# A two-layer attention and mixture-of-experts kernel: one slab's experts weighed on ScalarE out of PSUM, halved inverse sums stacked, and the steps put in another order without a loop

## The reference

```python
bias = einsum('bijd,dh->bhij', ln(x), Wb)                 # 4 heads, same for every row r
q, k, v = (ln(x) @ W).reshape(b, n, n, h, dh)             # W = Wq, Wk, Wv; dh = 32
sim = einsum('brihe,brjhe->brhij', q, k) * dh**-0.5 + bias[:, None]
attn = softmax(where(mask, sim, -1e9))
o = einsum('brhij,brjhe->brihe', attn, v)
x = x + (o * sigmoid(ln(x) @ Wg)) @ Wo
t = tokens(x)
p = softmax(ln(t) @ router_w + router_b)
top_p, top_i = top_k(p, 2);  top_p /= sum(top_p)
t = t + sum_k top_p[k] * (ln(t) @ expert_w[top_i[k]] + expert_b[top_i[k]])
```

## Time and profile before

| what | value |
|---|---|
| median of 3 runs | 878.78 us (878.75 to 878.98) |
| the profiled execution's own time | 878.26 us |
| its span, first to last instruction | 876.5 us |
| busy share of the span: PE, PEld, DVE, ACT, POOL | 92%, 61%, 86%, 57%, 74% |
| phase 1 and tables | 0 to about 97.8 us |
| first and last `exponent` of part 0 | 109.52 and 805.10 us |
| granted TensorE clock, 828 to 876.5 us | 0.51 of full speed |

### The profile page before, as it was taken

The page is one execution under the profiler, slowest core; times in us unless marked ns, Lnnn a source line. Parts: engine busy times, 40 slices in busy tenths (PEclk is TensorE's granted clock), DMA queues, the critical chain, the costliest instruction groups (busy, mean ns, idle before and its releaser), DMA issues.

```text
span 876.5 us, 40872 instructions
## 1 busy us (share of the span) xinstructions
PE 802.0 (92%) x15532; PEld 534.2 (61%) x15532; DVE 753.1 (86%) x1818; ACT 500.5 (57%) x1049; POOL 644.2 (74%) x1029
## 2 busy tenths in 40 slices
PE   1999679999999999999999999999999999999643
PEld 1899345666666666666666666666666666666411
DVE  8998545899999999999899998999999999998754
ACT  3887245655665566655665566655565566665220
POOL 6995002487788877887788878888788877888786
PEclk9999999999999999999999999999999999999955
DMA  4563100111110100101011100101011100100000
GB/s 118 193 200 137 39 25 22 37 39 35 34 56 30 37 30 30 52 30 37 30 45 37 37 30 30 52 30 37 30 44 38 37 30 30 52 25 18 17 15 16
DMA packets 32461, 40.82 MB, mean 47 GB/s; under 512 B 6288, under 2 KB 27280, under 8 KB 32400
## 3 DMA queue, kind: packets, MB, share of 16 engines
q1 hardware_dynamic: 31920, 39.95, 14.0%
q10 hardware_dynamic: 480, 0.02, 0.0%
HBM read 13.74 MB, written 6.55 MB: 23 GB/s over the span
## 4 chain that ended last, share of the span: by engine, by line
PE 67%; POOL 11%; issue 10%; DVE 9%; ACT 2%; DMA 0%; POOLq 0%; DVEq 0%
PE psS L1117 11%; PE psS L1092 6%; PE psS L1124 5%; DVE rinv L841 3%; POOL ln_s L375 3%; PE ps_x L1174 3%; PE ps_m L1174 3%; PE psS L1136 2%; PE ps_x L1177 2%; PE psS L1097 2%; PE ps_m L1177 2%; PE ps_o L1249 2%; POOL xn L378 2%; PE ps_x L1148 2%; PE ps_x L1250 2%
## 5 line engine op out<-in xcount | busy, mean ns | idle before, releaser
L825 DVE TENSOR_REDUCE negm<-psS 128x12 f16<-128x1920 f32 x80 | 145.7, 1821 | 16.2 <-PE psS L1097 9.0
L428 POOL TENSOR_TENSOR add<-prod 128x256 f32<-128x256 f32 x160 | 116.9, 730 | 4.3 <-DVE prod L943 2.1
L375 POOL TENSOR_TENSOR ln_s<-ln_s,half 128x5 f32<-128x5 f32 (+1 forms) x60 | 86.2, 1436 | 37.1 <-DVE ln_s L881 29.7
L433 POOL TENSOR_TENSOR add<-add 128x128 f32<-128x128 f32 x200 | 92.0, 460 | 3.1
L394 POOL TENSOR_TENSOR xc<-x,ln_s 128x320 f32<-128x320 f32 x40 | 29.3, 731 | 87.9 <-DVE ln_s L874 87.9
L545 ACT ACTIVATE pt_a<-psS 128x1280 f32<-128x1280 f32 x40 | 49.5, 1238 | 67.5 <-PE psS L1126 67.5
L545 ACT ACTIVATE pt_b<-psS 128x1920 f32<-128x1920 f32 x40 | 70.8, 1771 | 13.8 <-PE psS L1136 13.7
L435 POOL TENSOR_TENSOR ymix<-add 128x64 f32<-128x64 f32 x200 | 64.1, 321 | 15.7
L1092 PE MATMUL psS<-bm,ident 128*128 128x480 f16 (+1 forms) x320 | 68.0, 335 | 6.6 <-ACT pt_b L545 2.1
L416 POOL TENSOR_TENSOR og_lo<-og,og_hi 128x320 f16<-128x320 f32 x80 | 63.4, 793 | 10.5 <-ACT og_hi L582 9.9
L1117 PE MATMUL psS<-bt_hi,ident 128*128 128x320 f16 (+1 forms) x320 | 67.7, 334 | 3.3 <-issue 2.6
(11 more groups left out here) (267 smaller groups left out, 2921.2 us busy)
## 6 DMA issues: line engine op xcount, KB each, us to landing
xin<-in_x SPq DMA_DIRECT2D x20, 320.0 KB, 3.0
xs_all<-xs_pair SPq DMA_DIRECT2D x20, 320.0 KB, 2.5
xs_q<-xs_all SPq DMA_DIRECT2D x40, 160.0 KB, 2.1
xs_v<-xs_all SPq DMA_DIRECT2D x40, 160.0 KB, 2.1
xin<-in_x SPq DMA_DIRECT2D x40, 160.0 KB, 2.2
out<-res SPq DMA_DIRECT2D x40, 160.0 KB, 1.8
w_raw<-in_expert_w SPq DMA_DIRECT2D x2, 128.0 KB
eb_raw<-in_expert_b SPq DMA_DIRECT2D x15, 2.0 KB
```

Of the source, the lines that this page charges most:

```text
L375: pool.tensor_tensor(ln_s[a][:, 3, 0:w], ln_s[a][:, 2, 0:w], half[:, 0:w], ALU.pow).then_inc(own, 1)
L428: pool.tensor_tensor(add1[t % 2][:], prod_of(t)[:, 0:4, :], prod_of(t)[:, 4:8, :], ALU.add).then_inc(mix_step[t], 1)
L433: pool.tensor_tensor(add2[t % 2][:], add1[t % 2][:, 0:2, :], add1[t % 2][:, 2:4, :], ALU.add).then_inc(mix_step[t], 1)
L825: dve.tensor_reduce(negm[c][:, :, 0:slots], psS[:, :, 0:slots * N].rearrange("i h (s j) -> i h s j", s=slots), AX.X, ALU.max, negate=True) ...
```

## The change

**Slab 2.** `keep_expert` is gone. ACT's new `weigh_kept` reads the PSUM bank of slab 2 itself: eight activations (one per expert, 64 columns each) with the share `coef[:, 2, e]` as scale, a column of one value per partition. It waits for `share` 5, as POOL's did. POOL's multiply of `kept` is gone. The factor 1/16 now sits in `coef` (`share` 1 multiplies by 16 before the reciprocal), so `weigh` becomes a plain product and `share` 6 and 7 multiply by 16.

**Inverse sums.** `row_one` and `rest_one` have each row's ones twice, so `row_sums` gives each sum on two partitions. `rinv_high` is two activations, `rinv_s = sign * rinv` and `rinv_u = upper * rinv` (per-partition scales), and `rinv_low` one subtraction, `rinv_hl = rinv_u - rinv_s`: the tile has high halves on some partitions and low halves on others. `row_to_all` has ones at both, so `spread_inverse` is two matmuls for two rows instead of four. Its constants cost one more select on POOL, eight more small fills and three more small instructions on DVE, once.

**Order.** All five `step` lists are new, with other banks and offsets; steps -2 to 44 are all written out, without a loop, and there is one more step at the end. SP loads xs_q one step earlier and stores one step later.

```diff
-        FIRST, LOOP, LOOP_END, LAST = -2, 7, GROUPS - 3, GROUPS + 4
+        FIRST, LAST = -2, GROUPS + 5
-            for n in range(FIRST, LOOP):
-                step(n, n % 2)
-            pairs_loop(eng, step, LOOP, LOOP_END)
-            for n in range(LOOP_END, LAST):
+            for n in range(FIRST, LAST):
                 step(n, n % 2)
...
-                if third_on(n + 3): load_xq(n + 3, b)
+                if third_on(n + 4): load_xq(n + 4, a)
-                if on(n - 4): store(n - 4, a)
+                if on(n - 5): store(n - 5, b)
...
             def rinv_low(g):
                 pool.wait_ge(rh_done, g + 1)
-                pool.tensor_tensor(rinv_lo[:], rinv[:], rinv_hi[:], ALU.subtract).then_inc(rl_done, 1)
+                for c in range(2):
+                    need(pool, rb_done[c], g)
+                pool.tensor_tensor(rinv_hl[:], rinv_u[:], rinv_s[:], ALU.subtract).then_inc(rl_done, 1)
-            def weigh_kept(g, t):
-                pool.wait_ge(kept_done[t], g + 1)
-                pool.wait_ge(rt_tail, 7 * g + 5)
-                pool.tensor_tensor(kept[:], kept[:], coef[:, t, :].unsqueeze(2).broadcast_to([P, E, D]),
-                                   ALU.mult).then_inc(prod_done[t], 1)
...
             def rinv_high(g):
-                act.activation(rinv_hi[:], rinv[:], ACT.Copy).then_inc(rh_done, 1)
+                act.activation(rinv_s[:], rinv[:], ACT.Copy, scale=sign[:, 0:1])
+                act.activation(rinv_u[:], rinv[:], ACT.Copy, scale=upper[:, 0:1]).then_inc(rh_done, 1)
...
-            def keep_expert(g, t, bank):
+            def weigh_kept(g, t, bank):
                 act.wait_ge(e_done[t], g + 1)
+                act.wait_ge(rt_tail, 7 * g + 5)
...
-                act.activation(kept[:], bank[:].rearrange("p (e c) -> p e c", e=E), ACT.Copy, scale=1.0 / UP).then_inc(kept_done[t], 1)
+                for e in range(E):
+                    i = act.activation(kept[:, e, :], bank[:, D * e:D * e + D], ACT.Copy, scale=coef[:, t, e:e + 1])
+                i.then_inc(prod_done[t], 1)
...
+                prep(dve.tensor_reduce(upper[:], fold[:, 0:RG], AX.X, ALU.add))
+                prep(dve.tensor_scalar(sign[:], upper[:], -2.0, 1.0, ALU.mult, ALU.add))
+                prep(dve.tensor_scalar(upper[:], upper[:], -1.0, 1.0, ALU.mult, ALU.add))
...
             def spread_inverse(g, c, bank):
-                    mm(o, lhsT=row_to_all[:, 2 * c + s, :], rhs=rinv_hi[:], start=True, stop=False)
-                    end = mm(o, lhsT=row_to_all[:, 2 * c + s, :], rhs=rinv_lo[:], start=False, stop=True)
+                    end = mm(o, lhsT=row_to_all[:, 2 * c + s, :], rhs=rinv_hl[:], start=True, stop=True)
...
             def experts(g, a, t, bank):
-                take(bank, kept_done[t] if t in KEPT else prod_done[t], g + 1)
+                take(bank, prod_done[t], g + 1)
```

More of the change, by code:

```diff
@@ L1267, in step @@
                 b = 1 - a
-                if not isinstance(n, int) or n == LOOP_END:
-                    last[id(psS)] = max_done[1], n + 1
-                    last[id(ps_o)] = lg_done, n - 2
-                    last[id(ps_r)] = prod_done[3], n - 3
-                    last[id(ps_m)] = qkl_done[0][1], n + 2
-                    last[id(ps_x)] = qkl_done[1][1], n + 2
-                if on(n): scores(n, a, 0)
-                if on(n - 4): experts(n - 4, a, 4, ps_o)
-                if on(n): turn_max(n, 1, ps_r)
@@ L1278, in step @@
-                if later(n + 1): project_qk(n + 1, b, 0, 0, ps_m)
-                if on(n - 1): attend(n - 1, b, 1, ps_x)
-                if on(n - 4): turn_coef(n - 4, ps_o, banks16[0])
-                if on(n + 1): max_scores(n + 1, b, 0)
-                if on(n): project_v_rest(n, a, ps_r)
-                if on(n - 1): attend(n - 1, b, 0, ps_m)
-                if on(n + 1): project_gate(n + 1, b, 1, ps_x)
-                if on(n - 2): project_out(n - 2, ps_o)
-                if on(n + 1): project_gate(n + 1, b, 0, ps_r)
@@ L1287, in step @@
-                if on(n - 3): experts(n - 3, b, 2, ps_x)
-                if on(n): scores(n, a, 1)
-                if on(n - 4): expert_bias(n - 4, ps_m)
-                if on(n - 1): spread_inverse(n - 1, 1, ps_r)
-                if on(n - 3): experts(n - 3, b, 0, ps_x)
-                if on(n - 3): experts(n - 3, b, 1, ps_o)
-                if on(n): project_v(n, a, ps_m)
-                if on(n - 1): spread_inverse(n - 1, 0, ps_r)
+                if on(n): scores(n, a, 0)
+                if on(n - 1): attend(n - 1, b, 0, ps_x)
@@ new lines, in step @@
+                if on(n): turn_max(n, 1, ps_o)
+                if on(n - 5): expert_bias(n - 5, ps_r)
+                if on(n + 1): max_scores(n + 1, b, 0)
+                if on(n - 2): project_out(n - 2, ps_x)
+                if on(n + 1): project_gate(n + 1, b, 0, ps_o)
+                if on(n - 4): turn_coef(n - 4, ps_m, banks16[3])
+                if on(n - 1): attend(n - 1, b, 1, ps_r)
+                if on(n + 1): project_v_rest(n + 1, b, ps_o)
+                if on(n - 1): spread_inverse(n - 1, 0, ps_m)
@@ new lines, in step @@
+                if on(n): scores(n, a, 1)
+                if on(n - 1): spread_inverse(n - 1, 1, ps_o)
+                if on(n - 3): experts(n - 3, b, 1, ps_x)
+                if on(n - 3): experts(n - 3, b, 0, ps_m)
+                if on(n - 3): experts(n - 3, b, 2, ps_r)
+                if on(n - 3): experts(n - 3, b, 3, ps_o)
+                if on(n): row_sums(n, a, ps_x)
+                if later(n + 2): project_qk(n + 2, a, 0, 0, ps_m)
+                if on(n + 1): turn_max(n + 1, 0, ps_r)
@@ L1295, in step @@
+                if on(n + 1): project_gate(n + 1, b, 1, ps_o)
                 if on(n + 1): max_scores(n + 1, b, 1)
+                if on(n - 2): turn2(n - 2, a, ps_r, banks16[2])
+                if on(n): project_v(n, a, ps_x)
+                if on(n - 3): experts(n - 3, b, 4, ps_o)
+                if on(n - 2): router(n - 2, a, ps_r)
                 if later(n + 2): project_qk(n + 2, a, 1, 0, ps_m)
-                if on(n): row_sums(n, a, ps_x)
-                if on(n + 1): turn_max(n + 1, 0, ps_r)
@@ L1299, in step @@
-                if on(n - 2): turn2(n - 2, a, ps_o, banks16[0])
-                if later(n + 2): project_qk(n + 2, a, 0, 1, ps_m)
-                if on(n - 3): experts(n - 3, b, 3, ps_r)
-                if later(n + 2): project_qk(n + 2, a, 1, 1, ps_x)
-                if on(n - 2): router(n - 2, a, ps_o)
+                if later(n + 2): project_qk(n + 2, a, 0, 1, ps_x)
+                if later(n + 2): project_qk(n + 2, a, 1, 1, ps_r)
             pe.wait_ge(wb_ready, 1)
```

146 lines of the change are left out of this document (74 added, 72 removed).

## The result

The changed kernel takes **858.41 us** in the median of four runs (858.04 to 860.74); the kernel before, run beside it, 878.88 (878.75 to 879.07). The ratio is 0.9771, 95% interval 0.9756 to 0.9787: faster by 20.5 us. The forecast was 862.3 (854 to 875), so the direction and the range held and the size was 3.9 us short.

A forecast was written before the change was run, and what follows sets the result against it. The prediction took TensorE to bound phase 2, VectorE 1.3 us a step behind. Its terms, -3.7 - 9.9 - 9.2 + 10.8 - 2.2 + 0 - 3.0 + 0.7 = -16.5, gave a median of 862.3 us, range 854 to 875.

The forecast's parts named there:

- 4 new waits: TensorE waits at router for keep_xs2, second gate for slab 3's bank, row_sums for exponent: together 0.30 us a step, +10.8.
- 5 shapes: Changes of TensorE's array shape, with two joints no row shows: -0.06 us a step, -2.2, ends -3 and +4.5.
- 6 slab 2: Eight scaled activations on ScalarE take 1.8 us; turn_max waits for their bank with room up to 1.9: 0.
- 7 tail: GpSimd loses its 1.05 us multiply: off the path in full steps, saved in each of three last steps, -3.0 us.
- 8 head: Once before phase 2, VectorE runs three more small instructions, some 0.2 us each: +0.7 us.
- point 4b: TensorE's second gate needs the bank of slab 3's experts, which VectorE frees 0.07 us late.
- A: VectorE takes over and scores waits for row_max: 871.7 us, or 876; chance 0.17 shared with two other rivals.
- B: TensorE's new waits at router, second gate and row_sums are hidden: 851.5 us; chance 0.07.
- C: Slab 2's eight ScalarE activations do not overlap, so turn_max holds TensorE's queue 1.1 us a step: 902 us; chance 0.08.
- C': Slab 2's eight ScalarE activations take 2.0 us, so TensorE waits 0.13 us a step: 867 us; chance 0.13.
- D: Written-out steps run short of instructions, costing 0.35 us a step: 875 us; chance 0.17 shared with two other rivals.
- E: Stalls move but the step stays at 17.86 us, bound elsewhere: 872 us; chance 0.17 shared with two other rivals.

The follow-up runs named there:

- experiment 1: The kernel before with steps 7 to 36 written out instead of looped, nothing else changed: 875.09 us, ratio 0.995.
- experiment 6: The changed kernel with the first two of slab 2's eight activations cut into halves, so ten activations: 864.96 us, ratio 0.9842.
- experiment 4: The changed kernel with slab 2 copied by ScalarE and multiplied on GpSimd again, order otherwise as changed: 877.9 us, ratio 0.9977.
- experiment 9: The changed kernel with project_qk ahead of slab 4's experts and router, and small moves on VectorE, ScalarE, SP and TensorE: 866.58 us, ratio 0.9862.
- experiments 2: The kernel before with only the stacked inverse sums (two matmuls instead of four in spread_inverse), old order, loop and slab 2: 877.68 us, ratio 0.9984.
- experiment 5: The changed kernel's order with inverse sums unstacked and slab 2 copied by ScalarE and weighed on GpSimd: 878.33 us, ratio 0.9994.
- experiment 7: The changed kernel with an unused 128x640 fill on VectorE in each step, ahead of row_max of part 1: 869.56 us, ratio 0.9888.
- experiment 3: The changed kernel with the inverse sums unstacked again (eight matmuls), all else as changed: 868.21 us, ratio 0.9877.
- 8: The changed kernel with TensorE's router one call later, behind project_qk of the group after next: 859.54 us, ratio 0.9767.

## Why the prediction was right, and where it was off

By its own points, per step unless said otherwise (from the written-out kernel of experiment 1, 17.85, to 17.47: -0.38):

| point | forecast | measured |
| --- | --- | --- |
| 1 loop | -3.7 us in all | -4.1 (experiment 1) |
| 2 four matmuls | -0.28 | 4 x 0.069 = -0.28; undone in the new order +9.8 us |
| 3 wait for `rinv` | -0.26 | -0.27 (that joint 0.482, pace 0.216) |
| 4 new waits | +0.17, +0.07, +0.06 | +0.17, 0, +0.05 |
| 5 shapes | -0.06 | about -0.06, not measured by itself: what is left of the -0.38 |
| 6 slab 2 | eight in 1.8, room 1.9 | 1.75, room 1.97 (experiment 6) |
| 7 tail | -3.0 us | -3.8 us |
| 8 head | +0.7 us | -0.5 us |

**Right** were the bound and the terms. TensorE set the pace; its two holes went as said; the router's wait came where and as long as it was worked out. The two joints that no row had shown, `scores` to `attend` and `attend` to `project_v_rest`, are 0.16 and 0.12 us from start to start. The rule of the Trainium skill, Perfetto Trace Analysis (Identifying the Most-Contended Engine), by which TensorE at 65% weight load would not be the bound, is again not borne out: that share is 397/600 = 66% after the change too, and putting four matmuls back cost 0.22 of their 0.28 us a step.

**The step that failed by size** is point 4b: the second gate was to wait 0.07 for VectorE's weighing of slab 3, and does not. 0.07 x 36 = 2.5 us of the 3.9 that were missing. The walk had VectorE's release too late: by the rows in experiment 4 the bank is free 0.16 - 0.06 = 0.10 before the gate needs it. The wait is real once VectorE is later (0.21 at this same gate in experiment 4). The tail and the head gave another 0.8 and 1.2, each read from one trace; the loop's 0.4 lies inside the interval of experiment 1. That is more than 3.9; the falls of the clock described below, which no term held, took some of it back. Against the forecast span of 860.0 the profiled execution's 859.0 looks nearer than the account was: 3.2 us of it are such falls, and that they made up for the rest is luck. The head's first `exponent` stands at 109.06 us against 109.52, but in the written-out kernel with the old head at 111.26, so 1 to 2 us there move from program to program, and the +0.7 can't be judged.

The tail became shorter, by the mechanism named as far as the traces show. VectorE's `attention_out`, its last three starts in the timeline:

```profile
796.86 0.49 DVE L865 SCALAR_TENSOR_TENSOR x<-ps_x,xin 128x320 f32<-128x320 f32 x1 [2.81 <-POOL base L438]
813.50 0.49 DVE L865 SCALAR_TENSOR_TENSOR x<-ps_x,xin 128x320 f32<-128x320 f32 x1 [2.81 <-POOL base L438]
829.69 0.49 DVE L865 SCALAR_TENSOR_TENSOR x<-ps_x,xin 128x320 f32<-128x320 f32 x1 [1.99 <-POOL base L438]
```

They are 16.64 and 16.19 apart; before it was 17.23 and 17.24. It still waits for GpSimd each time, on a shorter chain. From the last `exponent` to the end of the span it is 67.6 us, against 71.4 before and 71.8 in experiment 4, with the multiply back on GpSimd. The multiply is not all that sets it: in experiment 9, with the same list on GpSimd, the same starts are 17.09 and 17.00 apart and the tail is 69.4. What makes that difference is open.

**A statement that was wrong although the sum was not** is in point 7, "In full steps that is off the path", with point 6's 0. Together the two points give the move 3.0 us; undoing it cost 19.5, of which 4.2 lie in the tail, because without it the new order waits for GpSimd and a bank, 0.39 a step. The sum came out because the walk had already been made over the whole new lists, with the move in them. So the points of such a sum are a bookkeeping of differences between two programs, not what each edit is worth. The loop's point had its value alone too (experiment 1); the four matmuls' had not (experiments 2 and 5).

**The rivals.** A (VectorE takes over) did not come. VectorE had 0.35 us of room at bank ps_r (experiment 7), and even without it `scores` did not wait for `row_max`, as A had said. B (waits hidden) was half true, for the gate. C and C' are out, with 0.22 us to spare. D is out by experiment 1. E, a step that stays near 17.86, is what either the order alone or the order with stacking does; slab 2's move makes the difference.

One thing stays open: where the walk goes wrong in experiments 7 and 9, for which it gave 17.93 and 17.49 us a step and 17.71 and 17.58 were measured. Laid end to end, lists with fixed durations hit one step of these runs (17.69 in experiment 3) and missed the others by 0.1 to 0.2 us, 3 to 8 us in all. That is enough for a 20 us change and useless for a 2 us one.

## What to carry to other kernels

Before counting removed work on the bounding engine as gain, look for the other engine's long instruction that runs under it (here an exponential of 1.77 us): unless the order puts other work there, the gain can turn into a wait of nearly the same length. In a list in which each bank is handed round within the step, the same part can be worth 1.5, 0.4 or 9.8 us (the stacking), 10.1 or 19.5 (slab 2's move), depending on what stands around it, so price the whole new list and test parts by undoing them in it, one at a time and together. A wait at one member of a chain (copy, `router`, `logits`, bank, `project_qk`) was not removed by moving one member, in both orders tried; it came back at the next joints.

## What the runs showed of the hardware

**TensorE's clock in the first steps.** The profiled execution of the changed kernel has 19.97 us between its first two `exponent`s, where the kernel before has 16.56. Its windows there:

```profile
114.00:117.50 3.50, 3.36 (x28) 1.63 (x32) 0.26 (x2) 0.17 (x1) 0.00 (x0) 0.51 0.00 0
121.00:124.30 3.30, 3.30 (x42) 2.34 (x33) 1.08 (x1) 0.31 (x2) 0.00 (x0) 0.50 0.00 0
```

and those of experiment 5, the same order without the two parts:

```profile
114.00:117.50 3.50, 2.88 (x96) 1.78 (x96) 0.36 (x2) 0.60 (x2) 0.00 (x0) 1.00 0.02 5
121.00:124.30 3.30, 2.88 (x34) 1.77 (x32) 2.71 (x3) 1.96 (x6) 0.00 (x0) 1.00 0.00 0
```

The granted clock falls to its lower level (1.2 GHz) twice. In the first window both work on the same list, and TensorE gets through 28 matmuls where the other gets through 96; by the second they are no longer at the same place in it. The distance of the first two `exponent`s is 16.77 us in the profiled executions of experiments 5 and 9, without a fall (17.18 in that of 7, which has the fill), 18.38 in those of 3, 6 and 8, 19.91 in that of 4, and 19.97 here: about 1.6 us for each fall. From 110 to 114 us, ahead of the first, TensorE had been busy for 2.12 of 4 us at the full clock, but for the same 2.12 in experiment 5, where no fall came, so what decides it is open. The spans of the other three runs, 2.3 to 2.7 us shorter, fit one or two falls less. This was in no term of the sum: 3.2 of the profiled execution's 859.0 us are these two falls.

**Activations in a row.** One line's instructions (ns min/median/max, first and last start):

```profile
L619 ACT ACTIVATE kept<-ps_r,coef x320: 306/337/372, 172.9 to 847.3; 128x64 f32<-128x64 f32 x160
```

They take 0.31 to 0.37 us at a distance of 0.20, so they overlap by 0.11 to 0.17. The Trainium skill, ScalarE: Activation LUTs (What ACT_TABLE_LOAD costs), gives an overlap of about 93 ns, from which the prediction's estimate of 2.0 us for the eight was made. The trace has 1.75. A per-partition scale made the 128x160 activation of the inverse 0.43 us long. The plain one of the kernel before took 0.32 (groups by line, before and after):

```profile
L576 ACT ACTIVATE rinv_hi<-rinv 128x160 f16<-128x160 f32 x40 | 12.8, 321 | 0.0
```

```profile
L570 ACT ACTIVATE rinv_s<-rinv,sign 128x160 f16<-128x160 f32 x40 | 17.1, 428 | 0.0
```
